# One ScalarE SiLU function, and exponential and logarithm from one table set, in a one-core decoder layer

## The reference

```python
xp, z = jnp.split(xz, 2, axis=-1)
xc = _silu(_causal_depthwise_conv(xp, conv_w, conv_b))
Bm, Cm = jnp.split(xc @ W_x, 2, axis=-1)
dt = jax.nn.softplus(xc @ W_dt + b_dt)
A = -jnp.exp(A_log)
y = _selective_scan(xc, dt, A, Bm, Cm, D)
y = y * _silu(z)
return y @ W_out
```

## Time and profile before

| | before |
|---|---|
| median of 3 runs | 1624.06 us |
| the profiled execution's own time | 1627.51 us |
| its span, first to last instruction | 1625.7 us |
| busy: TensorE / VectorE / ScalarE / GpSimd | 77% / 87% / 58% / 60% |
| mean granted TensorE clock | 0.902 |

### The profile page before, as it was taken

How to read it: one execution, slowest core, us unless ns; L and a number is a source line. 1 busy time by engine, 2 the same in 40 slices (tenths; PEclk the granted TensorE clock), 3 DMA queues, 4 the chain that set the end, 5 groups by cost and what they waited for, 6 DMA issues and landing times. The chain is left out here.

```text
span 1625.7 us, 24035 instructions
## 1 busy us (share of the span) xinstructions
PE 1246.4 (77%) x5942; PEld 852.6 (52%) x5942; DVE 1412.4 (87%) x1861; ACT 950.8 (58%) x1401; POOL 972.3 (60%) x529
## 2 busy tenths in 40 slices
PE   4756667779787868898777868788777777886797
PEld 2344444655455545665355545566345555565475
DVE  6589999797799999988699999989689999983697
ACT  2555444244777767524777767814777867722564
POOL 1298888312789878521689878721488978820000
PEclk9879999889798989999799989999889989997699
DMA  7111111401121211311112113221111211220111
GB/s 229 41 46 40 52 58 40 157 1 54 48 75 53 72 59 58 113 42 54 40 46 71 48 53 104 81 76 34 47 59 46 71 46 59 84 101 27 45 60 52
DMA packets 75758, 103.30 MB, mean 64 GB/s; under 512 B 9213, under 2 KB 52614, under 8 KB 75663
## 3 DMA queue, kind: packets, MB, share of 16 engines
q1 hardware_dynamic: 70508, 98.41, 19.1%
q10 hardware_dynamic: 5154, 3.78, 0.7%
HBM read 83.22 MB, written 18.96 MB: 63 GB/s over the span
## 5 line engine op out<-in xcount | busy, mean ns | idle before, releaser
L1804 PE MATMUL ps<-ident,work 128*128 128x128 f32 x1536 | 304.4, 321 | 214.4 <-DVE stage L1404 72.8
L1366 DVE TENSOR_TENSOR_SCAN work<-ps,work 128x1024 f32<-128x1024 f32 x192 | 438.4, 2283 | 27.7 <-ACT ps L966 20.2
L1804 PEld LDWEIGHTS ps<-ident,work 128*128 128x128 f32 x1536 | 191.8, 159 | 350.2 <-DVE stage L1404 124.6
L966 ACT ACTIVATE ps<-dt,a_neg 128x1024 f32<-128x1024 f32 x256 | 285.6, 1118 | 135.6 <-DVE work L1366 85.4
L719 POOL TENSOR_TENSOR work<-dtu,b_bc 128x1024 f32<-128x1024 f32 x128 | 301.8, 2385 | 50.4 <-PE ps L1804 46.5
L1404 DVE SCALAR_TENSOR_TENSOR stage<-ps,c_tok,stage 128x512 f32<-128x512 f32 x384 | 272.2, 733 | 22.2 <-PE ps L1804 20.1
L1826 PE MATMUL ps<-w,work 128*128 (+1 forms) x1024 | 249.5, 389 | 1.8 <-DVE work L1539 1.8
L1826 PEld LDWEIGHTS ps<-w,work 128*128 128x128 f32 x1024 | 195.9, 195 | 38.2 <-DVE work L1539 2.6
L735 POOL TENSOR_TENSOR stage<-stage,work 128x512 f32<-128x512 f32 x128 | 160.7, 1277 | 53.1 <-ACT work L982 53.1
L1776 PE MATMUL ps<-nfT,w 128*128 128x512 bf16 x512 | 165.8, 423 | 33.7 <-DVE work L1472 19.9
L719 POOL TENSOR_TENSOR work<-dtu,w_out 128x1024 f32<-128x1024 f32 x64 | 149.3, 2353 | 47.0 <-PE ps L1804 47.0
(11 more groups left out here) (169 smaller groups left out, 2017.0 us busy)
## 6 DMA issues: line engine op xcount, KB each, us to landing
b_bc<-b_rows SPq DMA_DIRECT2D x32, 512.0 KB, 3.9
w_out<-b_rows SPq DMA_DIRECT2D x32, 512.0 KB, 4.4
wbc<-combine_rows SPq DMA_DIRECT2D x64, 256.0 KB, 3.7
work<-z_rows SPq DMA_DIRECT2D x8, 1024.0 KB, 6.4
z_rows<-mix SPq DMA_DIRECT2D x24, 256.0 KB, 2.7
stage<-in_x SPq DMA_DIRECT2D x8, 512.0 KB, 4.3
xt<-in_x SPq DMA_DIRECT2D x8, 512.0 KB, 3.8
x_rows<-xt SPq DMA_DIRECT2D x4, 1024.0 KB, 4.3
```

The costliest lines, as they stand in the source:

```text
L966: act.activation(decay_in(d, alone, opening), dt[:, d, :], ACT.Exp, scale=a_neg[:, bass.ds(it * 2 + (d * N + hf * (N // 2) + par), 1)]).th ...
L1366: dve.tensor_tensor_scan(h, decays, h, 0.0, ALU.mult, ALU.add).then_inc(scan_done, 1)
L1804: mm = pe.transpose(ps[:, a % HT_BANKS, d * P:(d + 1) * P], slot(par, d)[:, a * P:(a + 1) * P], ident[:, :])
```

## The change

ScalarE applies Silu itself, in place for the convolved input and without the scale of 0.5 for the gate. VectorE's `silu` and `gate` are gone, with their 4 and 8 instructions a row, and so are the halvings of the convolution weights, of their bias and of the output weights, the store of the latter, and the buffer `tanh`. The output weights come from the input tensor each row, where they lie in rows of 1 KB. GpSimd and VectorE wait for `gate_ready` before the gated products. The softplus's table loads go: one set that has both functions is loaded once a phase. As Silu is in a set of its own, loads are added around it.

```diff
-                def silu_tanh(d):
+                def silu(d):
                     act.wait_ge(conv_done, b * CT * KTAPS + (d + 1) * KTAPS)
-                    act.activation(tanh[:, d % 2, :], xc[:, d, :], ACT.Tanh).then_inc(tanh_done, 1)
+                    act.activation(xc[:, d, :], xc[:, d, :], ACT.Silu).then_inc(xc_ready, 1)
...
                 def soft_logs(*batch):
-                    act.preload_act_table(ACT.Ln)
...
-                    act.preload_act_table(ACT.Exp)
...
                     for d in (0, 1):
-                        silu_tanh(d)
+                        silu(d)
                         conv_in(d + 2)
+                    if r is not None:
+                        act.preload_act_table(ACT.Exp)
                 if r is not None:
                     if b is not None:
                         for c in halves:
                             score_exps(c)
+                        act.preload_act_table(ACT.Silu)
...
                     for d in (2, 3):
-                        silu_tanh(d)
+                        silu(d)
+                    act.preload_act_table_set("natural_log_exp_and_others")
...
                     opening_decay(3)
+                    act.preload_act_table(ACT.Exp)
...
-                        act.activation(dt[:, d, c * HALF:(c + 1) * HALF], soft[:, c * CT + d, :], ACT.Tanh,
-                                       scale=0.5).then_inc(gate_tanh, 1)
+                        act.activation(dt[:, d, c * HALF:(c + 1) * HALF], soft[:, c * CT + d, :], ACT.Silu
+                                       ).then_inc(gate_ready, 1)
...
-                def silu(d):
-                    dve.wait_ge(tanh_done, b * CT + d + 1)
-                    dve.scalar_tensor_tensor(xc[:, d, :], tanh[:, d % 2, :], 1.0, xc[:, d, :],
-                                             ALU.add, ALU.mult).then_inc(xc_ready, 1)
...
-                        dve.scalar_tensor_tensor(dt[:, d, cols], dt[:, d, cols], 1.0, soft[:, c * CT + d, :],
-                                                 ALU.add, ALU.mult)
...
-                    sp.dma_start(w_out[:, :, :].rearrange("p k n -> p (k n)"), w_outd).then_inc(w_out_loaded, 16)
+                    sp.dma_start(w_out[:, :, :], t["W_out"].rearrange("(k p) n -> p k n", p=P)).then_inc(w_out_loaded, 16)
```

More of the change, by code:

```diff
@@ L135, in decoder_layer @@
         bc_sb = work[:, 6912:6912 + QUARTER]
-        TANH_AT = 8192
-        NORM_AT = TANH_AT - 8 * TT
+        NORM_AT = 8192 - 8 * TT
         stats = work[:, NORM_AT:NORM_AT + 6 * TT].rearrange("p (a n) -> p a n", n=6)
-        mv = work[:, NORM_AT + 6 * TT:TANH_AT].rearrange("p (a n) -> p a n", n=2)
+        mv = work[:, NORM_AT + 6 * TT:NORM_AT + 8 * TT].rearrange("p (a n) -> p a n", n=2)
         assert 6912 + S <= NORM_AT
-        tanh = work[:, TANH_AT:TANH_AT + 2 * S].rearrange("p (r t) -> p r t", r=2)
         xcT = dt[:, 0:DK, :]
@@ L288, in decoder_layer @@
         out_ready = sem("out_ready")
-        gate_tanh = sem("gate_tanh")
+        gate_ready = sem("gate_ready")
         z_ready = sem("z_ready")
@@ L500, in _ @@
                              allow_slow_non_contiguous=True).then_inc(w_first, 16)
-            for dst, name in ((w_x, "W_x"), (w_dt, "W_dt"), (w_out, "W_out")):
+            for dst, name in ((w_x, "W_x"), (w_dt, "W_dt")):
                 sp.dma_start(dst[:, :, :], t[name].rearrange("(k p) n -> p k n", p=P)).then_inc(w_early, 16)
@@ L763, in loop @@
                         ph.wait_taken(pool, ("Y", d, c))
+                        wait_apart(pool, gate_ready, b * CT * NH + c * CT + d + 1)
                         cols = slice(c * HALF, (c + 1) * HALF)
@@ L789, in scale_weights @@
             def scale_weights():
[L791 removed]
+                act.wait_ge(w_early, 3 * 16)
                 act.activation(a_neg[:, :], a_log, ACT.Exp).then_inc(act_scaled, 1)
@@ L879, in score_exps @@
                                        ).then_inc(exp_probs, 1)
-                if b is not None:
+                if b is None:
+                    act.preload_act_table(ACT.Exp)
+                else:
                     for c in halves:
@@ L973, in loop @@
                     act.wait_ge(shift_set, 3)
-                    act.wait_ge(dve_scaled, 5)
+                    act.wait_ge(dve_scaled, 3)
                 def evict(hf, it, par):
@@ L1010, in keep_z, with gate_silus @@
                                    ).then_inc(z_kept, 1)
-                def gate_tanhs(c, tiles):
+                def gate_silus(c, tiles):
                     wait_apart(act, z_loaded[c], b * 16 + 16)
                     for d in tiles:
-                        act.activation(dt[:, d, c * HALF:(c + 1) * HALF], soft[:, c * CT + d, :], ACT.Tanh,
-                                       scale=0.5).then_inc(gate_tanh, 1)
+                        act.activation(dt[:, d, c * HALF:(c + 1) * HALF], soft[:, c * CT + d, :], ACT.Silu
+                                       ).then_inc(gate_ready, 1)
                 def late_linear(hf, it, par):
@@ L1119, in loop @@
                     turns(act, body)
-                gate_tanhs(0, range(2))
+                gate_silus(0, range(2))
                 evict(1, ITS, 0)
@@ L1123, in loop @@
                     clip(state(bp, 1, ITS, 0) * 2)
-                gate_tanhs(0, range(2, CT))
-                gate_tanhs(1, range(CT))
+                gate_silus(0, range(2, CT))
+                gate_silus(1, range(CT))
                 if bp is not None:
@@ L1292, in phases @@
                         convolve(d)
-                    for d in (2, 3):
-                        silu(d)
                 if r is not None:
@@ L1549, in loop @@
                     ph = phase_after(b)
-                    gate(0, range(2))
                     if bp is not None:
@@ L1554, in loop @@
                         accumulate(1, ITS, 0, a)
-                    gate(0, range(2, CT))
                     skip(ph, 0)
@@ L1562, in loop @@
                         finalize(1, 1)
-                    gate(1, range(CT))
                     skip(ph, 1)
@@ L1716, in job_b @@
                 if r is None:
-                    pe.wait_ge(w_early, 4 * 16)
+                    pe.wait_ge(w_early, 3 * 16)
                 ph.wait_bank(pe, job)
@@ L1789, in loop @@
                 if bp is not None:
-                    pe.wait_ge(dve_scaled, 5)
+                    pe.wait_ge(dve_scaled, 3)
                 def transpose_states(w, par, tiles):
```

20 lines of the change are left out of this document (3 added, 17 removed).

## The result

The changed kernel takes 1599.65 us (median of 4 runs, 1597.53 to 1603.63), the kernel before 1624.05 us in the runs beside them (1622.07 to 1624.16). The ratio is 0.9851, 95% interval 0.983 to 0.9872: 24.2 us faster (20.8 to 27.6), where 20.9 was forecast. The profiled execution took 1600.42 us with a span of 1598.6, 27.1 less than the profiled one of before.

The account below looks back on a forecast made before the run. VectorE was busiest (87%), but its work counted only where on the path, with TensorE bounding many places. Phase 0 -6.3, phase 1 -1.8, phase 2 -6.5, phase 3 -5.9, last -0.4: -20.9 from 1624.06 gives 1603.2, range 1598 to 1608.

Parts of the forecast that it names:

- Softplus, phases 1 to 3: Router's input and last step in phases 1 to 3: removed loads bring G and the last step forward, -2.9 us each.
- From G on, TensorE bounds: S4 to S7 are behind it: Softplus, phases 1 to 3: behind G TensorE sets the time, and loads of batches two and three are beside this.
- allowance of 5 us: TensorE's granted clock, averaging 0.902, may be more or less where waits shorten: 5 us either way.
- Phase 0: First phase, no attention beside it: -3.7 from SiLU ahead of B and -2.6 from softplus loads, -6.3 us.
- Gate: End of loop up to the norm: -3.4 us before phase 2, -2.8 before phase 3, +1.3 before phase 1.
- TensorE isn't moved: Gate before phase 2: TensorE's output product still starts at 692.08 and ends at 707.8.
- SiLU, phases 1 to 3: Middle of the phase: new load ahead of score exponentials eats VectorE's gain, SiLU 2 and 3 hidden, -0.2 us each.
- Loops: Loops between the phases: given no part in the change, 0 us; another length would be a sign of being wrong.
- More of VectorE's work counting: Rival, chance 0.15: TensorE comes forward with VectorE, so gates and SiLU give 11 us more, 1592.
- A second 1.28 at each added load: Rival, chance 0.15: switches to or from Silu's set cost an extra idle gap at 7 places, 9 us back, 1612.
- A dear load of Silu's set: Rival, slower, chance 0.04: loads of Silu's set or back far dearer; at 6 us a load, 1650.
- the compiler put back no load: Rival, chance 0.03: a function missing from a set makes the compiler restore 12 loads on ScalarE, 1612.

Follow-up runs that it names:

- softplus alone: The kernel before with one table set for exponential and logarithm in softplus, SiLU and gate still tanh products: 1608.68 us, ratio 0.99.
- silu_only: The kernel after with the old loads around every pair of logarithms, so SiLU and gate alone on ScalarE: 1617.43 us, ratio 0.9955.
- scores-first kernel: The kernel after with SiLU of tiles 0 and 1 behind the copies of the transposed probabilities in phases 1 to 3: 1598.34 us, ratio 0.9831.
- gate_only: The kernel before with only the gate's Silu on ScalarE and the exponential's set loaded at phase start: 1623.83 us, ratio 0.9974.
- before_warm: The kernel before with three useless products in TensorE's wait ahead of G in phases 1 to 3: 1620.55 us, ratio 0.9964.
- early_load: The kernel after with the load of Silu's set ahead of the wait for z at each loop's end: 1599.64 us, ratio 0.9834.
- the three with two loads: The kernel after with two loads put back ahead of the first logarithms, phases 1 to 3: 1612.75 us; plus five useless products 1613.11; plus three 1608.83.
- two_loads: The kernel after with two table loads put back ahead of the first pair of logarithms in phases 1 to 3: 1612.75 us, ratio 0.9939.

## Why the prediction was right, point by point

**Right as a whole.** 1603.2 was forecast with a range of its own from 1598 to 1608, 1599.65 measured. The measured gain is 24.2 (20.8 to 27.6); 20.9 is at the edge of that, so the runs of the whole change alone don't prove it too small; softplus alone does (-16.3, -20.0 to -12.5, against -11.3). In the traces the sum is -27.05 against -20.9: the softplus of phases 1 to 3 gave 7.0 more than forecast, and all other terms together 0.9 less.

**Softplus, phases 1 to 3: the mis-sized term.** The mechanism was right: the two loads reach the router's input, G starts behind S3, the last step gains its 0.44. The term was -2.9 a phase and measured -4.64, -4.80 and -6.31. The forecast said "From G on, TensorE bounds: S4 to S7 are behind it" and took their durations as fixed. They weren't: 1.51 + 1.70 + 2.89 = 6.1 us came from the clock of S4 and S5. What is left, 3.13, 3.10 and 3.42, is near the forecast. The 6.1 has a part of chance: with the S4 and S5 of silu_only, which has the same wait (8.57, 8.61 and 8.65 us), it would have been 4.5. The trace of before had both signs in it, the 2.81 us of idle time and 8.6 to 10.0 us for S4 and S5 where S6 and S7 take 7.13 behind them, and I used only the first. My allowance of 5 us "either way" for the clock was of about the right size, in the wrong place: it belonged to this stretch, with a sign.

**Phase 0: -6.3, measured -5.95.** TensorE's wait for SiLU fell from 14.22 to 10.61, by 3.6 where 3.7 was given, and B to `dtu` gives 2.4 where 2.6 was. The mark itself moves by more between executions (see the end), but these two parts don't: the seven traces with this phase 0 that are named there have 10.61 or 10.62, and 2.1 to 2.9.

**Gate: -3.4, -2.8 and +1.3, measured -3.58, -2.52 and +2.08.** The details differ from the forecast, the sum hardly. VectorE now waits 3.07 for ScalarE's clipping in place of 1.33, since this stands behind the load and the evictions, and 0.25 for TensorE's transposes in place of 1.92; so before phase 2 `skip` comes 1.8 earlier relative to the end of the loop (1.2 forecast), and the cast 1.2 (1.0 forecast), where it waits for the product. Timeline of after, VectorE at the end of loop 1 (compare):

```profile
668.62 0.69 DVE L1447 SCALAR_TENSOR_TENSOR work<-ps,work 128x512 f32<-128x512 f32 x1 [3.07 <-ACT ps L1033]
669.56 2.91 DVE L1386 SCALAR_TENSOR_TENSOR stage<-ps,c_tok,stage 128x512 f32<-128x512 f32 x4 [0.25 <-PE ps L1773]
678.11 0.69 DVE L1402 CAST mix<-ps 128x512 bf16<-128x512 f32 x1 [0.49 <-PE ps L1795]
```

"TensorE isn't moved" was not quite so: against the end of the loop its output product starts 1.1 us earlier before phase 2 (681.99 us, where 692.08 was) and 0.4 later before phase 3, and it waits for GpSimd's gated product (2.49 us). Before phase 1 the norm waits for the transfer of x, and the +2.08 is one execution's: the other traces with the load in this place give +0.4 to +2.6, most of them 1.5 to 2.1.

**SiLU, phases 1 to 3: -0.2 each, measured -0.57, -0.27 and +0.45.** The new load eats what VectorE gives, and the scores-first kernel shows it from the other side: without it in the way the exponentials come 1.8 us earlier. SiLU 2 and 3 are hidden behind V; VectorE's wait for V grew from 0.48 to 2.2, not to several us:

```profile
739.02 0.42 DVE L1207 TENSOR_TENSOR xt<-xt,ps 128x256 f32<-128x256 f32 x1 [0.92 <-PE ps L1681]
740.75 0.42 DVE L1207 TENSOR_TENSOR xt<-xt,ps 128x256 f32<-128x256 f32 x1 [1.31 <-PE ps L1681]
```

**Loops: 0, measured +1.40, -1.27, -0.84 and -0.31.** They add up to -1.0, but the "0" was an assumption, and loops of another length were among the forecast's signs of being wrong. Loop 0 is longer by 1.7 with SiLU alone and 0.9 with softplus alone, and by 0.1 to 0.3 in the two kernels whose phase 0 is unchanged (gate_only, before_warm). The granted clock in its first 200 us is 0.93 before, 0.91 in those two, 0.89 with softplus alone and 0.88 in after and with SiLU alone. Whether the lower clock makes the loop longer, and what lowers it, stays open, as do the gains of loops 1 and 2.

**The rivals.** More of VectorE's work counting falls by SiLU and gate alone (-7.3, where the forecast's own terms give -9.6 and the rival -14 or more). A second 1.28 at each added load falls by the rows: the load of 718.49 ends at 719.77 and the exponential starts at 719.78. By this the Trainium skill (ScalarE: Activation LUTs, section What ACT_TABLE_LOAD costs), which adds a drain of 1.38 us to each switch, isn't borne out here, also for the two sets that the trace of before didn't have; and two loads in a row cost 2.70 us in all, where an estimate by that rule is 5.3. A dear load of Silu's set falls by the groups (1283 ns), and the compiler put back no load.

## What to carry to other kernels

Where TensorE waits and then bounds, price the wait twice: its length, and what the clock behind it costs. Compare the duration of the jobs behind the wait with equal jobs elsewhere; here 2.55 us less idle time was worth 4.1 to 5.4. If the wait can't go, filling it with products that nobody reads gave back the second part in this kernel (5.9 us of 1624), as long as they fit: behind the two loads three products left a cost of 2.7 us a phase, and five, which didn't fit, left 3.9.

A table load was a plain 1.28 us instruction here, whichever set it brought: what it costs is decided by what waits for the instruction behind it. Before moving functions into one set, look where the new loads land. A load that stands ahead of a wait for a transfer is hidden in it; the one moved there (early_load) gave no gain that the runs can tell.

## What the runs showed beyond that

The `dtu` product of phase 0 stands at 77.7 to 81.5 us in the traces of seven kernels whose phase 0 is the same (after and its repetition, the three with two loads, scores first, early load): executions differ by up to 3.9 us before anything in which these kernels differ. Most of it lies ahead of TensorE's wait for SiLU, which begins at 30.2 to 33.4 us. Marks are compared from there on, and a quarter of a per cent between single executions proves nothing.

The slow S4 and S5 come in two sizes, 8.45 to 8.81 us in nine of the twelve phases and about 10.0 in three, with clocks of about 0.82 and 0.71, behind the same idle time of 2.8 to 3.0 us and in the same program (before, gate_only and two_loads have one of the large ones each, in phases 3, 1 and 2). What the idle time costs isn't fixed by its length alone, and what sets it stays open.
